# Adding a saved residual into an image in SBUF: accumulating DMAs in place of loads and engine additions

## The chip, the cores and the metric

The kernel runs on one core of one Trainium2 chip. The metric is device time in microseconds (us) of one execution of the whole program. The core has TensorE (PE in the profile, with its weight loads as PEld), VectorE (DVE), ScalarE (ACT), GpSimd (POOL) and SyncE (SP), and 16 DMA engines. Every array here is float32.

## The reference, cut to what matters

The image x is 4 x 48 x 128 x 128 (batch, channels, rows, columns). Four layers follow each other, each on a group-normalised copy of x and added to x:

```python
x = x + attention(_gn(x), ...)      # layer 0
x = x + scans(_gn(x), down1, right1, left1)   # layer 1
x = x + scans(_gn(x), down2, right2, left2)   # layer 2
x = x + gated_mlp(_gn(x), ...)      # layer 3

def step(w, b):                     # one step of a scan
    def f(carry, inp):
        nxt = inp + conv1d(carry, w, b)     # 5 taps, 48 -> 48 channels
        return (nxt, nxt)
    return f
# scans: down over the rows, up, right over the columns, left: 127 steps each
# _gn: 16 groups of 3 channels, mean and variance over channels, rows and columns
```

What matters here is the place between layer 1 and layer 2. The scans of layer 1 leave their output in the image; `x` from before layer 1 is then added to it, the sum is kept for the residual of layer 2, and its group statistics and normalisation feed the scans of layer 2.

## The kernel before

**Layout.** `image` is one SBUF tensor of 128 partitions by 32768 float32 columns. The 48 channels sit twice in it: partitions 0 to 47 (`LO`) hold one half of the pixels (even columns or rows), partitions 64 to 111 (`HI`) the other. Partitions 48 to 63 are a gap that holds zeros. The columns fall into four parts of `IMG` = 8192 columns, numbered t = 0 to 3. Parts 0 and 1 together hold batch elements 0 and 1, parts 2 and 3 hold batch elements 2 and 3. A part is four chunks of `CHUNK` = 2048 columns (`PER` = 4).

**DRAM copies.** `saved[0]` holds x from before layer 1. It is written while layer 0 ends, and its DMAs (L381, L388) are waited for before anything reads it. `saved[1]` receives x from before layer 2 and is read back, block by block, after the scans of layer 2 (L431, L539 and the DVE loop at the end of the scans).

**Between the scan layers.** Each engine runs its own instruction list and waits on semaphores. Layer 1 ends with the last swap copies on DVE (L1220). Then:

- SP loads `saved[0]` chunk by chunk into four buffers `back[0..3]` in the tensor `work` (`bring`, L398: two DMAs of 384 KiB a chunk, one for `LO`, one for `HI`). The four chunks of part 0 are loaded early, during the scans of layer 1. A chunk of part t+1 is loaded once the addition of the same chunk of part t has freed its buffer.
- DVE adds chunks 0 and 1 of each part (L1230), GpSimd adds chunks 2 and 3 (L529). Additions count into `s_kept_v` and `s_kept_p`.
- DVE takes the statistics of each part: 16 instructions of 512 columns (L1047, `take_stats`), the last four of them behind GpSimd's second addition. After parts 0 and 1, and again after parts 2 and 3, `group_norm` turns statistics into scale and shift: aggregation on DVE (L1054), two small matmuls (L805), a square root on ACT (L600) and a few small DVE instructions up to `gn_shift` (L1068).
- SP stores each part to `saved[1]` (`save_columns`, L403): parts 0 to 2 whole, two DMAs of 1536 KiB each, part 3 in two halves of two DMAs of 768 KiB each. SP works in program order, so the store of part t is issued behind the loads of part t+1.
- ACT (L695) and DVE (L1251) normalise the image in place, each part only once its store has landed (`s_save`). ACT takes parts 0 and 1 and most of part 3, DVE takes part 2 and the first quarter of part 3. Then PE starts the scans of layer 2 (L923).

Before the first load, SP waits for `s_back_gap`: four memsets of the gap lanes of `back` on GpSimd (L497), done during the scans of layer 1.

Of the kernel before, what the change touches and what calls it, by code (L numbers as in the profile page):

```python
# [97 lines left out]
def build(nc, x, qkv_t, v_w, dw_t, dw_v, proj_t, temp, scan_w, scan_b,  # L98
          w1, b1, gamma, beta, gdw, gdw_b, gpw_t, gpw_b, w2, b2,
          ident_c, group_half_c, group_flat_c, saved, flat, out):  # L100
    with ExitStack() as ctx:
# [114 lines left out]
        s_gate_w = sem("s_gate_w")  # L216
        s_back_gap = sem("s_back_gap")
        s_gate_zero = sem("s_gate_zero")
# [35 lines left out]
        s_back = [sem(f"s_back{i}") for i in range(PER)]  # L254
        s_kept_v = sem("s_kept_v")
        s_kept_p = sem("s_kept_p")
        s_res = sem("s_res")
# [80 lines left out]
        def _(sp):  # L338
# [53 lines left out]
            for i in range(PARTS):  # L392
                sp.wait_ge(s_part[i], 32)
            sp.wait_ge(s_back_gap, PER)

            def bring(c):
                for half, rows in enumerate((LO, HI)):
                    sp.dma_start(back[c % PER][rows, :],  # L398
                                 saved[0][half, :, c * CHUNK:(c + 1) * CHUNK]).then_inc(s_back[c % PER], 16)

            def save_columns(b, c0, c1):
# [3 lines left out]

            for c in range(PER):
                bring(c)
            for b in range(NB - 1):
                for m in range(PER):
                    if m < VCH:  # L410
                        sp.wait_ge(s_kept_v, b * VCH + m + 1)
                    else:
                        sp.wait_ge(s_kept_p, b * (PER - VCH) + m - VCH + 1)
                    bring((b + 1) * PER + m)
                save_columns(b, 0, IMG)
            sp.wait_ge(s_kept_v, NB * VCH)
            save_columns(NB - 1, 0, VCH * CHUNK)
            sp.wait_ge(s_kept_p, NB * (PER - VCH))
            save_columns(NB - 1, VCH * CHUNK, IMG)
            for t in range(NB):  # L420
# [43 lines left out]
        def _(pool):  # L464
# [29 lines left out]
            for g in range(2):  # L494
                pool.wait_ge(s_state[g], 1)
            for m in range(PER):
                nc.gpsimd.memset(back[m][32:HALF, :], 0.0).then_inc(s_back_gap, 1)  # L497
            pool.wait_ge(s_back_gap, PER)

            pool.wait_ge(s_const, 16 * N_CONST)  # L500
# [22 lines left out]
            for g in range(2):  # L523
                pool.wait_ge(s_state[g], PASSES * STEPS + 1)
            with pool.Fori(0, NB) as b:
                for m in range(VCH, PER):
                    pool.wait_ge(s_back[m], b * 32 + 32)
                    dst = image[0:P, ds(b * IMG + m * CHUNK, CHUNK)]
                    nc.gpsimd.tensor_tensor(dst, dst, back[m], ALU.add).then_inc(s_kept_p, 1)  # L529

# [3 lines left out]
            with pool.Fori(0, NB // 2) as bp:  # L534
                with pool.Fori(0, NBLK // PER) as q:
                    for m in range(PER):
                        pool.wait_ge(s_back[m], bp * (NBLK * 8) + q * 32 + (32 * NB + 32))
                        pool.wait_ge(s_flat[m % 2], bp * (NBLK * 16) + q * 64 + (m // 2 * 32 + 32))
                        natural(nc.gpsimd, bp, q, m, 1, 1).then_inc(s_res_p, 1)  # L539
# [499 lines left out]
        def _(dve):  # L1039
# [182 lines left out]
            for layer in range(2):  # L1222
                if layer:
                    for pair in range(2):
                        for s in range(2):
                            t = 2 * pair + s
                            for m in range(VCH):
                                dve.wait_ge(s_back[m], t * 32 + 32)
                                dst = image[0:P, t * IMG + m * CHUNK:t * IMG + (m + 1) * CHUNK]
                                v.tensor_tensor(dst, dst, back[m], ALU.add).then_inc(s_kept_v, 1)  # L1230
                            for m in range(PER):
                                if m < VCH:
                                    dve.wait_ge(s_kept_v, VCH * t + (m + 1))
                                else:
                                    dve.wait_ge(s_kept_p, (PER - VCH) * t + (m - VCH + 1))
                                for q in range(2):
                                    for c in range(2):
                                        k0 = (2 * m + c) * BLK
                                        src = img(slice(0, P), 2 * pair + q, s, slice(k0, k0 + BLK), slice(0, J2))
                                        last = take_stats(P, 2 * pair + q, s * NBLK + 2 * m + c,  # L1240
                                                          src.rearrange("p k j -> p (k j)"))
                            last.then_inc(s_stat, 1)
                        if pair == 0:
                            dve.wait_ge(s_stat, X_STATS + NB + 2)
                            group_norm(4, P, NSTAT, 0, 2)
# [50 lines left out]
            with dve.Fori(0, NB // 2) as bp:  # L1296
                with dve.Fori(0, NBLK // PER) as q:
                    for m in range(PER):
                        dve.wait_ge(s_back[m], bp * (NBLK * 8) + q * 32 + (32 * NB + 32))
                        dve.wait_ge(s_flat[m % 2], bp * (NBLK * 16) + q * 64 + (m // 2 * 32 + 32))  # L1300
# [150 lines left out]
```

## Time and profile before

| | before |
|---|---|
| median of 3 runs | 2922.65 us (2920.05 to 2925.99) |
| the profiled execution | 2917.19 us |
| its span, first to last instruction | 2915.4 us |
| mean granted TensorE clock | 0.937 |
| PE busy | 2487.5 us (85%) |
| DVE busy | 1630.1 us (56%) |
| ACT busy | 1095.3 us (38%) |
| POOL busy | 250.1 us (9%) |
| moved by DMA | 130.12 MB |

"Busy" is the time in which an engine executes instructions. The span is one profiled execution, and all durations and moments below are taken from it, counted from the span's start. In a view of windows the columns are the window, its length, busy time and number of instructions for PE, PEld, DVE, ACT and POOL, the granted TensorE clock (1.00 is 2.4 GHz, 0.50 is 1.2 GHz), the mean busy share of the 16 DMA engines, and the GB/s that they moved. A share slightly above 1 comes from packets whose recorded times overlap.

### The profile page before, as it was taken

What the parts mean: (1) busy time and instruction counts of PE and PEld (TensorE: products, weight loads), DVE (VectorE), ACT (ScalarE), POOL (GpSimd) and SP (SyncE); (2) the same over time, 40 slices, a digit from 0 to 9 for tenths busy, and PEclk for the clock granted to TensorE, in tenths of its full rate; (3) what the DMA queues carried; (4) which work ended last, traced back from release to release, by engine and by line L of the source; (5) the groups of instructions that cost most, each with busy time, mean ns of one, the idle gap of its engine ahead of it and who ended that gap; (6) DMA issues with size and microseconds to landing.
All of it is one profiled execution on the core that took longest, in us unless ns stands there. A gap on an engine that the chain in (4) does not pass through costs nothing.

```text
span 2915.4 us, 46645 instructions
## 1 busy us (share of the span) xinstructions
PE 2487.5 (85%) x18076; PEld 2175.9 (75%) x18076; DVE 1630.1 (56%) x3797; ACT 1095.3 (38%) x2617; POOL 250.1 (9%) x244
## 2 busy tenths in 40 slices
PE   2999999999999899999999906999999998005876
PEld 2989949949943699999999906999999998002443
DVE  2323223223232455885568875558855788776564
ACT  3533353353357344444444423444444444002221
POOL 1000000000000440000000040000000000454110
PEclk9999999999999999999999957999999999558898
DMA  8840000003001400000000094000000000683223
GB/s 147 146 74 2 1 1 1 1 0 88 1 0 44 87 1 1 2 1 1 1 1 1 1 249 97 1 1 1 1 1 1 1 2 1 192 283 87 87 86 87
DMA packets 51667, 130.12 MB, mean 45 GB/s; under 512 B 9121, under 2 KB 34049, under 8 KB 44897
## 3 DMA queue, kind: packets, MB, share of 16 engines
q1 hardware_dynamic: 48352, 113.92, 16.4%
q10 hardware_dynamic: 2976, 13.34, 1.6%
q8 instruction: 138, 2.26, 0.3%
q14 instruction: 73, 0.59, 0.1%
q0 software_dynamic: 128, 0.01, 0.0%
HBM read 76.91 MB, written 50.33 MB: 44 GB/s over the span
## 4 chain that ended last, share of the span: by engine, by line
PE 83%; DVE 6%; DMA 6%; issue 2%; ACT 1%; SPq 0%; POOL 0%; DVEq 0%; ACTq 0%; POOLq 0%
PE bank L923 17%; PE bank L924 15%; PE bank L926 15%; PE bank L830 13%; PE bank L884 11%; PE bank L845 3%; PE bank L835 3%; DMA flat_rows<-work 2%; PE bank L968 2%; DVE work L322 1%; PE bank L1026 1%; DMA work<-saved 1%; DMA work<-in_x 1%; DVE stats L1047 1%; PE bank L959 1%
## 5 line engine op out<-in xcount | busy, mean ns | idle before, releaser
L1210 DVE TENSOR_SCALAR bank<-image,scan_bias 112x128 f32<-112x128 f32 x2032 | 725.7, 358 | 416.0 <-ACT image L714 373.1
L714 ACT COPY image<-bank 112x128 f32<-112x128 f32 x2032 | 596.5, 294 | 787.7 <-PE bank L926 787.4
L923 PE MATMUL bank<-image,scan_wt 112*112 112x128 f32 x4064 | 818.2, 282 | 31.3 <-ACT image L695 16.4
L924 PE MATMUL bank<-image,scan_wt 112*112 112x126 f32 x4064 | 770.7, 271 | 0.0
L926 PE MATMUL bank<-image,scan_wt 112*112 112x126 f32 x4064 | 769.6, 270 | 0.0
L923 PEld LDWEIGHTS bank<-image,scan_wt 112*112 112x112 f32 x4064 | 556.2, 175 | 41.9 <-ACT image L695 26.9
L924 PEld LDWEIGHTS bank<-image,scan_wt 112*112 112x112 f32 x4064 | 581.3, 176 | 0.0
L926 PEld LDWEIGHTS bank<-image,scan_wt 112*112 112x112 f32 x4064 | 578.3, 176 | 0.0
L621 ACT ACTIVATE work<-image,gn_shift,gn_scale 48x567 f32<-48x567 f32 (+5 forms) x384 | 332.5, 899 | 344.6 <-PE bank L835 219.3
L830 PE MATMUL bank<-work 112*128 112x192 f32 x2304 | 424.0, 332 | 10.1 <-issue 10.1
L830 PEld LDWEIGHTS bank<-work 112*128 112x128 f32 x2304 | 375.3, 193 | 11.7 <-issue 11.2
L884 PE MATMUL bank<-work 112*112 112x512 f32 x768 | 331.3, 593 | 3.0 <-DVE work L1137 3.0
L884 PEld LDWEIGHTS bank<-work 112*112 112x112 f32 x768 | 135.3, 177 | 192.9 <-issue 189.6
L1105 DVE COPY work<-bank 128x384 f32<-128x384 f32 x128 | 71.3, 557 | 359.9 <-PE bank L835 276.7
L1047 DVE BATCH_NORM_STATS2 stats<-image 112x6 f32<-112x512 f32 (+2 forms) x240 | 152.9, 683 | 62.1 <-ACT image L593 43.7
L1158 DVE TENSOR_TENSOR image<-image,bank 112x512 f32<-112x512 f32 (+1 forms) x64 | 44.1, 689 | 236.7 <-PE bank L884 140.6
L805 PE MATMUL bank<-mean_var,group_flat 128*128 128x4 f32 x2 | 0.6, 366 | 165.4 <-DVE mean_var L1054 165.4
L322 POOL TENSOR_TENSOR work<-image,work 48x1024 f32<-48x1024 f32 x16 | 58.8, 3680 | 777.3 <-DVE image L1220 715.2
L805 PEld LDWEIGHTS bank<-mean_var,group_flat 128*128 128x128 f32 x2 | 0.5, 313 | 165.6 <-DVE mean_var L1054 165.6
L805 PE MATMUL bank<-mean_var,group_half 112*112 112x2 f32 (+2 forms) x12 | 2.5, 276 | 136.3 <-DVE mean_var L1054 136.3
L322 DVE TENSOR_TENSOR work<-image,work 48x1024 f32<-48x1024 f32 x48 | 98.6, 2053 | 28.1 <-DMA flat_rows<-work 26.5
L845 PE MATMUL bank<-work 128*96 128x96 f32 x1024 | 108.2, 248 | 3.8 <-DVE work L1105 3.8
(137 smaller groups left out, 1604.3 us busy)
## 6 DMA issues: line engine op xcount, KB each, us to landing
work<-saved SPq DMA_DIRECT2D x64, 384.0 KB, 8.5
saved<-image SPq DMA_DIRECT2D x10, 1536.0 KB, 21.7
flat_rows<-work ACTq DMA_DIRECT2D x32, 384.0 KB, 7.4
image<-flat_rows SPq DMA_DIRECT2D x4, 3072.0 KB, 14.3
out<-image SPq DMA_DIRECT2D x8, 1536.0 KB, 8.1
saved<-image SPq DMA_DIRECT2D x12, 768.0 KB, 10.1
band<-in_x SPq DMA_DIRECT2D x16, 384.0 KB, 5.9
work<-in_x SPq DMA_DIRECT2D x16, 384.0 KB, 6.1
```

The lines of the kernel that those rows point to most:

```text
L322: return eng.tensor_tensor(o[:, :, :, :, half], i0.rearrange("p g s k j -> p (g s) k j"), i1, ALU.add)
L621: last = nc.scalar.activation(dst.rearrange("p (k j) -> p k j", j=J2)[:, :, d[0]:d[1]], src, ACT.Identity, bias=gn_shift[part, b:b + 1], s ...
L714: nc.scalar.copy(line(g, along_w, at), state_bank(g, done)).then_inc(s_state[g], 1)
L830: last = mm(dst, (blk_z, blk_n)[buf][n % 2][:, o:o + 2 * J2], qk_w[buf][:, dy].rearrange("p a b -> p (a b)"), start=(t == 0), stop=(packed ...
L835: last = mm(dst[:, side * QK:(side + 1) * QK], blk_2[n % 2][:, side, sub, o:o + 2 * J2], qk_w2[:, side, :], start=False, stop=(side == 1))
L845: last = mm(bank_gram[0:QK, 0:QK], v, v, start=(i == 0 and c == 0), stop=(i == PAIRS - 1 and c == 3))
L884: last = mm(bank_out[sub][0:P, :], out_w[buf][:, dy, :], (blk_z, blk_n)[buf][n % 2][:, o:o + BLK * J2], start=(t == 0), stop=(t == len(pro ...
L923: mm(dst, wt[:, 1], src, start=False, stop=False, skip_group_check=True)
L924: mm(dst[:, 1:J2, :], wt[:, 0], src[:, 0:J2 - 1, :], start=False, stop=False, skip_group_check=True)
L926: mm(dst[:, 0:J2 - 1, :], wt[:, 2], src[:, 1:J2, :], start=False, stop=True, skip_group_check=True).then_inc(s_prod[g], 1)
L1047: return v.bn_stats(stat6[0:parts, b, ds(c * 6, 6)], src)
L1210: v.tensor_scalar(state_bank(g, done), line(g, along_w, src), scan_bias[:, 3 * layer + kind:3 * layer + kind + 1], None, ALU.add).then_inc ...
```

## The change

The loads of `saved[0]` into `back`, the additions on DVE and GpSimd, their semaphores and the memsets of the gap lanes are gone. In their place GpSimd issues 16 accumulating DMAs, all behind each other and without a wait between them, once layer 1 has ended: for each part t, for each half u of it (4096 columns), one for `LO` and one for `HI`. Each has `saved[0]` in DRAM as its source and the image in SBUF as its destination, adds the source to what stands there, and is 48 partitions x 4096 columns (768 KiB), cut into rows of 2048 elements (8192 bytes). Each half counts on its own semaphore `s_acc[2t+u]`. DVE waits for a half before the eight statistics instructions on it. SP waits for both halves of a part and stores it to `saved[1]`; part 3 is stored half by half, as before in two DMAs each. Since `bring` no longer counts on `s_back`, the later waits on it lose the term `32 * NB`.

```diff
--- before.py
+++ after.py
@@ -214,7 +214,6 @@
 
         s_const = sem("s_const")
         s_gate_w = sem("s_gate_w")
-        s_back_gap = sem("s_back_gap")
         s_gate_zero = sem("s_gate_zero")
         s_gate_const = sem("s_gate_const")
         s_pool = sem("s_pool")
@@ -252,8 +251,7 @@
         s_swap = sem("s_swap")
         s_tail = sem("s_tail")
         s_back = [sem(f"s_back{i}") for i in range(PER)]
-        s_kept_v = sem("s_kept_v")
-        s_kept_p = sem("s_kept_p")
+        s_acc = [sem(f"s_acc{i}") for i in range(2 * NB)]
         s_res = sem("s_res")
         s_res_p = sem("s_res_p")
         s_flat = [sem(f"s_flat{i}") for i in range(2)]
@@ -391,32 +389,18 @@
                 sp.wait_ge(s_save[t], 32)
             for i in range(PARTS):
                 sp.wait_ge(s_part[i], 32)
-            sp.wait_ge(s_back_gap, PER)
-
-            def bring(c):
-                for half, rows in enumerate((LO, HI)):
-                    sp.dma_start(back[c % PER][rows, :],
-                                 saved[0][half, :, c * CHUNK:(c + 1) * CHUNK]).then_inc(s_back[c % PER], 16)
-
             def save_columns(b, c0, c1):
                 for half, rows in enumerate((LO, HI)):
                     sp.dma_start(saved[1][half, :, b * IMG + c0:b * IMG + c1],
                                  image[rows, b * IMG + c0:b * IMG + c1]).then_inc(s_save[b], 16)
 
-            for c in range(PER):
-                bring(c)
-            for b in range(NB - 1):
-                for m in range(PER):
-                    if m < VCH:
-                        sp.wait_ge(s_kept_v, b * VCH + m + 1)
-                    else:
-                        sp.wait_ge(s_kept_p, b * (PER - VCH) + m - VCH + 1)
-                    bring((b + 1) * PER + m)
-                save_columns(b, 0, IMG)
-            sp.wait_ge(s_kept_v, NB * VCH)
-            save_columns(NB - 1, 0, VCH * CHUNK)
-            sp.wait_ge(s_kept_p, NB * (PER - VCH))
-            save_columns(NB - 1, VCH * CHUNK, IMG)
+            for t in range(NB):
+                for u in range(2):
+                    sp.wait_ge(s_acc[2 * t + u], 32)
+                    if t == NB - 1:
+                        save_columns(t, u * IMG // 2, (u + 1) * IMG // 2)
+                if t < NB - 1:
+                    save_columns(t, 0, IMG)
             for t in range(NB):
                 sp.wait_ge(s_save[t], saves(1, t))
 
@@ -493,10 +477,6 @@
 
             for g in range(2):
                 pool.wait_ge(s_state[g], 1)
-            for m in range(PER):
-                nc.gpsimd.memset(back[m][32:HALF, :], 0.0).then_inc(s_back_gap, 1)
-            pool.wait_ge(s_back_gap, PER)
-
             pool.wait_ge(s_const, 16 * N_CONST)
             pool.wait_ge(s_gate_w, 16 * N_GATE)
             n = 0
@@ -522,11 +502,17 @@
             pool.wait_ge(s_swap, 6 * K2)
             for g in range(2):
                 pool.wait_ge(s_state[g], PASSES * STEPS + 1)
-            with pool.Fori(0, NB) as b:
-                for m in range(VCH, PER):
-                    pool.wait_ge(s_back[m], b * 32 + 32)
-                    dst = image[0:P, ds(b * IMG + m * CHUNK, CHUNK)]
-                    nc.gpsimd.tensor_tensor(dst, dst, back[m], ALU.add).then_inc(s_kept_p, 1)
+            for t in range(2):
+                pool.wait_ge(s_save[t], 32)
+            for i in range(PARTS):
+                pool.wait_ge(s_part[i], 32)
+            for t in range(NB):
+                for u in range(2):
+                    for half, rows in enumerate((LO, HI)):
+                        dst, src = (r[:, t * IMG + u * IMG // 2:t * IMG + (u + 1) * IMG // 2]
+                                    for r in (image[rows, :], saved[0][half]))
+                        pool.dma_start(dst.rearrange("p (a n) -> p a n", n=CHUNK), src.rearrange("p (a n) -> p a n", n=CHUNK),
+                                       accum_op=ALU.add, max_dma_last_dim=8192).then_inc(s_acc[2 * t + u], 16)
 
             pool.wait_ge(s_swap, 2 * 6 * K2)
             for g in range(2):
@@ -534,7 +520,7 @@
             with pool.Fori(0, NB // 2) as bp:
                 with pool.Fori(0, NBLK // PER) as q:
                     for m in range(PER):
-                        pool.wait_ge(s_back[m], bp * (NBLK * 8) + q * 32 + (32 * NB + 32))
+                        pool.wait_ge(s_back[m], bp * (NBLK * 8) + q * 32 + 32)
                         pool.wait_ge(s_flat[m % 2], bp * (NBLK * 16) + q * 64 + (m // 2 * 32 + 32))
                         natural(nc.gpsimd, bp, q, m, 1, 1).then_inc(s_res_p, 1)
 
@@ -1224,15 +1210,9 @@
                     for pair in range(2):
                         for s in range(2):
                             t = 2 * pair + s
-                            for m in range(VCH):
-                                dve.wait_ge(s_back[m], t * 32 + 32)
-                                dst = image[0:P, t * IMG + m * CHUNK:t * IMG + (m + 1) * CHUNK]
-                                v.tensor_tensor(dst, dst, back[m], ALU.add).then_inc(s_kept_v, 1)
                             for m in range(PER):
-                                if m < VCH:
-                                    dve.wait_ge(s_kept_v, VCH * t + (m + 1))
-                                else:
-                                    dve.wait_ge(s_kept_p, (PER - VCH) * t + (m - VCH + 1))
+                                if m % 2 == 0:
+                                    dve.wait_ge(s_acc[2 * t + m // 2], 32)
                                 for q in range(2):
                                     for c in range(2):
                                         k0 = (2 * m + c) * BLK
@@ -1296,7 +1276,7 @@
             with dve.Fori(0, NB // 2) as bp:
                 with dve.Fori(0, NBLK // PER) as q:
                     for m in range(PER):
-                        dve.wait_ge(s_back[m], bp * (NBLK * 8) + q * 32 + (32 * NB + 32))
+                        dve.wait_ge(s_back[m], bp * (NBLK * 8) + q * 32 + 32)
                         dve.wait_ge(s_flat[m % 2], bp * (NBLK * 16) + q * 64 + (m // 2 * 32 + 32))
                         for a, half in ((0, 0), (0, 1), (1, 0)):
                             last = natural(v, bp, q, m, a, half)
```

## Rows read from the trace of the kernel before

**Rows 1.** The page: PE's busy line, and PE and DMA in 40 slices.

```profile
PE 2487.5 (85%) x18076; PEld 2175.9 (75%) x18076; DVE 1630.1 (56%) x3797; ACT 1095.3 (38%) x2617; POOL 250.1 (9%) x244
...
PE   2999999999999899999999906999999998005876
...
DMA  8840000003001400000000094000000000683223
```

**Rows 2.** Windows: scans of layer 1, the stretch between the layers.

```profile
1000.00:1600.00 600.00, 597.65 (x5329) 594.55 (x5328) 403.53 (x1189) 255.97 (x889) 53.68 (x100) 1.00 0.02 3
...
1673.40:1777.90 104.50, 2.14 (x8) 1.79 (x8) 72.70 (x99) 22.72 (x9) 41.43 (x8) 0.51 0.83 219
```

**Rows 3.** The chain that ended last, 1697 to 1778 us: start, length, what.

```profile
1697.81 22.16 DMA work<-saved
...
1729.26 17.58 DMA work<-saved
...
1751.50 4.50 POOL image L529
...
1756.38 14.79 DMA saved<-image
...
1774.33 3.07 ACT image L695
...
1777.94 0.74 PE bank L923 x2
```

**Rows 4.** Waits from 1660 to 1790 us: waiting line, releaser, total, times, longest.

```profile
POOL image L529 <- DMA work<-saved: 39.4, 3, 16.3
ACT image L695 <- DMA saved<-image: 26.8, 2, 17.5
...
DVE image L1230 <- DMA work<-saved: 13.3, 4, 8.0
```

**Rows 5.** Windows inside the stretch, and one of stores alone (668 to 692 us).

```profile
1677.00:1688.70 11.70, 0.00 (x0) 0.00 (x0) 11.70 (x11) 0.00 (x0) 10.91 (x2) 0.50 0.72 138
1684.00:1752.00 68.00, 1.07 (x4) 0.90 (x4) 49.17 (x72) 16.13 (x5) 28.58 (x7) 0.50 0.98 266
...
1720.00:1730.00 10.00, 0.00 (x0) 0.00 (x0) 9.51 (x13) 0.63 (x1) 7.38 (x2) 0.50 1.05 333
...
668.00:692.00 24.00, 24.00 (x184) 23.85 (x183) 9.11 (x23) 6.94 (x9) 0.00 (x0) 1.00 0.79 184
```

**Rows 6.** Groups of instructions from 1674 to 1778 us: busy us, mean ns.

```profile
L529 POOL TENSOR_TENSOR image<-image,work 112x2048 f32 x8 | 41.4, 5197 | 653.7 <-DVE image L1220 614.3 <-DMA work<-saved 39.4
L1047 DVE BATCH_NORM_STATS2 stats<-image 112x6 f32<-112x512 f32 x64 | 38.7, 676 | 5.8 <-POOL image L529 5.7
L1230 DVE TENSOR_TENSOR image<-image,work 112x2048 f32<-112x2048 f32 x8 | 22.4, 2824 | 13.3 <-DMA work<-saved 13.3
```

**Rows 7.** Loads of line 398 in the stretch: durations ns, first and last start.

```profile
L398 SPq DMA_DIRECT2D work<-saved x24: 302/614/4041, 1677.1 to 1735.3; - x24
```

**Rows 8.** Timeline: start, length, instruction, idle time before it.

```profile
1675.15 12.77 POOL L529 TENSOR_TENSOR image<-image,work 112x2048 f32 x2 [614.29 <-DVE image L1220]
...
1756.03 2.47 DVE L1047 BATCH_NORM_STATS2 stats<-image 112x6 f32<-112x512 f32 x4 [1.99 <-POOL image L529]
1758.54 1.03 DVE L1054 BATCH_NORM_AGGREGATE mean_var<-stats 112x2 f32<-112x96 f32 x2
...
1762.20 0.16 DVE L1068 SCALAR_TENSOR_TENSOR gn_shift<-gn_mean,gn_scale 112x2 f32<-112x2 f32 x1
```

**Rows 9.** GpSimd's timeline where it issues four small DMAs.

```profile
2610.83 0.71 POOL L548 DMA_DIRECT2D work<-in_w  x1 [0.72 <-POOL work L546]
2611.53 0.53 POOL L549 DMA_DIRECT2D work<-in_w  x1
2612.06 0.50 POOL L550 DMA_DIRECT2D work<-in_b  x1
```

**Rows 10.** DMA issues, whole span: count, KB each, median us to landing.

```profile
scan_wt<-in_scan_w SPq DMA_DIRECT2D x60, 9.0 KB, 1.7
...
work<-in_w POOLq DMA_DIRECT2D x2, 3.0 KB, 6.3
```

## The prediction, made before the changed kernel was run

> **What bounds the kernel now.** I read the page first, to see where PE is not busy, since PE carries the kernel: 85% busy, with full slices through both groups of scans and one hole near slice 24, where the DMA row stands at 9 and 4 [rows 1]. A window over the scans of layer 1 shows PE busy for 597.65 of 600 us and the DMA engines at 0.02 [rows 2]. The change touches nothing that runs there but memsets and early loads that PE does not wait for. So only the hole counts. It lasts from 1673.4 to 1777.9 us, 104.5 us in which PE does 2.14 us of work [rows 2].
>
> The second question is what fills the hole. DVE is busy for 72.7 us of it and POOL for 41.4, but the DMA engines for 0.83 of the whole [rows 2], and for 0.98 from 1684 to 1752 us, at 266 GB/s [rows 5]. The waits say the same: POOL waited 39.4 us for loads, DVE 13.3 us, and ACT 26.8 us for stores [rows 4]. The chain of waits through the hole runs over two loads of 22.16 and 17.58 us, a last addition on POOL that ends at 1751.50 + 4.50 = 1756.0, a store of 14.79 us, ACT's normalisation, and PE's start at 1777.94 [rows 3]. The reader is to see that the DMA engines are the bound of this stretch and that the additions are not.
>
> The bytes confirm it. 24 loads fall in the stretch [rows 7], each 384 KiB or 0.393 MB, together 9.44 MB; the four chunks of part 0 (3.15 MB) were loaded before it. The stores are 4 parts of 3.15 MB, 12.58 MB, of which three parts (9.44 MB) belong ahead of the last addition. 9.44 + 9.44 = 18.9 MB at 266 GB/s is 71 us, nearly all of the 81 us from 1675 to 1756.
>
> **The change part by part.**
>
> 1. It removes 8 additions on DVE, 22.4 us, and 8 on POOL, 41.4 us [rows 6]. They lie beside transfers. DVE's share never comes back as time unless the DMA engines get less to do, so I give the two nothing by themselves.
>
> 2. It removes 24 loads in the stretch, 9.44 MB, and adds 16 accumulating DMAs, 12.58 MB, all in the stretch: nothing can be fetched ahead, since the destination is the image that the scans still write. That alone is 3.15 MB more, 3.15/0.266 = 11.8 us.
>
> 3. The price of an accumulated byte is not in the trace. An accumulating DMA must read DRAM, read SBUF, add and write SBUF. From below it is one transfer, as a load is: 266 GB/s as in the saturated stretch [rows 5], or 333 GB/s as in its best 10 us [rows 5]. From above it is three passes (two reads and one write, none overlapped), each at 266 GB/s. I take two transfers, a load and a store of the same bytes, since that is what it does to SBUF; and since such traffic runs in both directions at once, I take for it the mixed window, 333 GB/s: 2 x 12.58 / 0.333 = 75.6 us. Reads in one direction alone run slower here: loads alone moved 138 GB/s at a share of 0.72, stores alone 184 at 0.79, which is some 190 and 230 GB/s if the engines were full [rows 5]. The three parts stored ahead of the last accumulation cost 9.44 / 0.266 = 35.5 us. Together 111.1 us of DMA time.
>
> The Trainium skill ("Collectives: The Full Stack", "Why ReduceScatter is half of AllGather") says that a DMA add is slowed not by the adding but by its two source reads, which share one ring, so that a reduce runs at half the rate of a copy. No row here shows an accumulate. By that rule on the 266 GB/s row the accumulations would take 12.58 / 0.133 = 94.6 us and the sum below would be 19 us more.
>
> 4. GpSimd now issues the DMAs. The additions on POOL began at 1675.15 [rows 8], so the first issue falls there. Issuing a small one took 0.71, 0.53 and 0.50 us [rows 9]; 16 of them at under 3 us each would be under 48 us, beside 111 us of transfers, so issue is hidden. But a small DMA from POOL took 6.3 us to land against 1.7 from SP [rows 10]. Those 4.6 us stand once at the front, where nothing covers them: before, the first chunks were already in SBUF. So the transfers begin at 1675.15 + 4.6 = 1679.8. SP waits for the last accumulation of a part before it stores it; later accumulations do not queue behind SP, so that wait holds back nothing but the store.
>
> 5. The last accumulation then lands at 1679.8 + 111.1 = 1790.9, against 1756.0 for the last addition: +34.9 us.
>
> 6. The tail. Before it was 1777.94 - 1756.0 = 21.9 us, with the store of 14.79 us in it [rows 3]. Now two things are different. DVE takes eight chunks of statistics after the last landing instead of four: 8 x 0.61 (2.47/4 in [rows 8]) = 4.9 us, and from the aggregation to gn_shift it is 1762.36 - 1758.54 = 3.8 us [rows 8], together 8.7, still under 14.8. And the earlier stores have had more time to drain, so that the last 1.57 MB may land faster than in 14.8 us, by at most 14.8 - 8.7 = 6.1. I take 3 us off.
>
> 7. The statistics of a part take 16 x 0.6 = 10 us, under the 28 us that a part's DMA work now takes; they stay hidden, also the group norm of parts 0 and 1 and ACT's first normalisation, which wait for stores that land long before the end. The four removed memsets and the early loads lie under the scans [rows 2]: nothing.
>
> Sum: +34.9 - 3 = +32 us in the hole. The profiled execution took 2917.19 us, the span and 1.8 us around it, and the median of the runs is 2922.65. I add the difference to the median: 2922.65 + 32 = 2954.7, say **2955 us**. Its own range: all the work at 333 GB/s gives 34.6/0.333 = 103.9 us and +22 with the full 6 us of the tail; all at 266 gives 130.1 us and +54 with none of it: 2944 to 2977 us.
>
> **The rivals.**
>
> - *One pass.* The accumulation costs what a load costs: 22.0 MB at 266 GB/s is 82.8 us, landing at 1762.6, +6.6 - 3 = +3.6 us, **2926 us**. For it: a load is short of the engines' full rate for some other reason than the reading (loads alone give only some 190 GB/s at a full share), so a second read might hide under it. Against it: the engines' recorded share was 0.98 already.
>
> - *One pass and better overlap: faster.* Two queues, POOL's and SP's, feed the engines at once, with transfers of 768 KiB and no stop to wait for a buffer. If one-pass accumulations and stores then ran at 333 GB/s throughout, 22.0/0.333 = 66.1 us, landing at 1745.9, -10.1 - 3 = -13 us, **2910 us**. It decides where the stores and accumulations together take under 76.2 us (1756.0 - 1679.8): with the stores at 266, where accumulated bytes run above 12.58/(76.2 - 35.5) = 309 GB/s. For it: the 10 us at 333. Against it: every byte is read twice, and the average of the saturated stretch is 266.
>
> - *Three passes.* The two reads and the write follow each other in each engine: 37.7/0.266 = 141.9 us, with the stores 177.4, landing at 1857.2: +101 - 3 = +98 us, **3021 us**. For it: loads alone, one partition half at a time, got only 138 GB/s; the accumulations go in that order too, a `LO` and then a `HI`, on one queue. Against it: nothing in the trace shows reads and writes in an engine excluding each other, and the mixed window is the fastest.
>
> - *GpSimd's issue sets the pace.* 16 DMAs would need over 7 us each. Against it the three rows at 0.5 to 0.7 us; it is within the chance of the slow case.
>
> **How the numbers follow.** Two transfers 50%, three passes or slower accumulation of other cause (+60 us and more) 25%, one pass 14%, faster 11%. Measurement tells apart about 0.2%, 5.8 us: faster is below 2916.8, slower above 2928.5. The faster case gives 0.11. The one-pass case is mostly within the bound: 0.12. The rest is slower: 0.77. The range leaves out the best of the faster case and the worst of the slow one: 2915 to 3025 us.
>
> **What would show it.** In the changed kernel's profile: the hole in PE some 136 us long, DMA share near 1 for over 100 us of it; DVE's busy time in the hole down from 72.7 to about 50 us, its idle time before L1047 put down to DMA; 16 issues on POOL of a few us at most; the last accumulation landing near 1791 us and PE's start some 19 us behind. The first landing tells the most: the first half of part 0 (1.57 MB) alone on the engines should land some 10 to 13 us after its issue. Under 9 us speaks for one pass, over 17 us for three. I am wrong if the accumulations do not fill the engines' time (a latency per row instead of a rate), if POOL's issues last 7 us or more, or if the stores and accumulations slow each other beyond the sum of their shares.

## The result and the profile after

The changed kernel takes 2975.03 us (median of 4 runs, 2961.16 to 2981.57) against 2923.1 us before (4 runs): a ratio of 1.0173 with a 95% interval of 1.0148 to 1.0198, which is 50.6 us more (43 to 58). The forecast was 2955 us and slower: the direction held, the extra time was 50.6 us where 32 were forecast, and the mechanism held in part. The profiled execution is the fastest of the four, 2961.16 us with a span of 2959.4, 44 us over the one before.

The page shows where the time went (PE and DMA in 40 slices, then two DMA queues with packets, MB and their share of 16 engines over the span). The rows of before are in [rows 1].

```profile
PE   2989999999999899999999603999999999005786
...
DMA  8830000012002100000000396000000000683222
...
q1 hardware_dynamic: 46304, 101.33, 14.5%
q0 software_dynamic: 1920, 12.59, 2.3%
```

The hole in PE near slice 24 is wider. 12.59 MB now go over GpSimd's queue (q0), which carried almost nothing before. Windows over the hole and its parts, with the columns of [rows 2]:

```profile
1674.70:1824.60 149.90, 2.13 (x8) 1.81 (x9) 49.71 (x88) 22.62 (x8) 14.93 (x16) 0.50 0.85 174
...
1679.00:1807.00 128.00, 1.07 (x4) 0.90 (x4) 36.08 (x65) 15.97 (x5) 10.63 (x12) 0.50 0.87 182
1679.00:1755.00 76.00, 1.07 (x4) 0.90 (x4) 21.54 (x41) 7.49 (x3) 10.63 (x12) 0.50 1.03 203
1755.00:1807.00 52.00, 0.00 (x0) 0.00 (x0) 14.54 (x24) 8.48 (x3) 0.00 (x0) 0.50 0.63 150
```

DVE's busy time falls from 72.7 us in [rows 2] to 49.7, as it should. The DMA engines move 182 GB/s while accumulations and stores share them, where loads and stores moved 266 [rows 5]. Their share is 1.03 in the first 76 us and only 0.63 in the last 52 us before the last landing; the prediction wanted it near 1 for over 100 us, and the hole 136 us long where it is 149.9. The waits from 1660 to 1830 us (the rows of before are [rows 4]):

```profile
DVE stats L1033 <- DMA image<-saved: 95.3, 8, 16.3
ACT image L681 <- DMA saved<-image: 15.3, 2, 13.1
```

DVE's and GpSimd's timelines, and the end of the chain of waits (start, length, what). The trace gives no name to an accumulation's landing there, "an unknown queue":

```profile
1674.69 14.93 POOL L514 DMA_DIRECT2D image<-saved  x16 [621.89 <-DVE image L1206]
...
1690.31 4.84 DVE L1033 BATCH_NORM_STATS2 stats<-image 112x6 f32<-112x512 f32 x8 [16.27 <-DMA image<-saved]
...
1807.15 4.84 DVE L1033 BATCH_NORM_STATS2 stats<-image 112x6 f32<-112x512 f32 x8 [13.42 <-DMA image<-saved]
```

```profile
1791.57 15.56 another core or an unknown queue
...
1807.50 10.03 DMA saved<-image
...
1820.94 3.14 ACT image L681
...
1824.61 0.74 PE bank L909 x2
```

Issuing all 16 DMAs cost GpSimd 14.93 us, 0.9 each. The first rows start moving at 1676.5, 1.8 us behind the first issue. The first half landed 15.6 us after its issue (1690.31 - 1674.69), the last at 1807.1 against 1756.0 for the last addition [rows 3], and PE starts 17.5 us behind that.

### The profile page after: what moved, and what is told of

Same layout as the page of the kernel before. It is cut to its first block, busy times and chain, and to the rows that moved or that the text cites. A ratio compares the mean times of both kernels' runs of the same rounds, so it can differ in the third digit from the quotient of the medians.

```text
span 2959.4 us, 46594 instructions
## 1 busy us (share of the span) xinstructions
PE 2491.4 (84%) x18076; PEld 2177.8 (74%) x18076; DVE 1608.3 (54%) x3789; ACT 1095.8 (37%) x2617; POOL 219.2 (7%) x248
## 3 DMA queue, kind: packets, MB, share of 16 engines
q0 software_dynamic: 1920, 12.59, 2.3%
## 4 chain that ended last, share of the span: by engine, by line
PE 82%; DVE 5%; DMA 5%; another core or an unknown queue 3%; issue 2%; ACT 1%; SPq 1%; POOL 0%; DVEq 0%; ACTq 0%; POOLq 0%
PE bank L909 17%; PE bank L910 15%; PE bank L912 15%; PE bank L816 13%; PE bank L870 11%; PE bank L831 3%; PE bank L821 3%; DMA flat_rows<-work 2%; PE bank L954 2%; DVE work L320 1%; PE bank L1012 1%; DMA work<-in_x 1%; PE bank L945 1%; DMA image<-saved 1%
```

## The experiments

Each was timed against the kernel before on the same chip; the third column is the ratio's excess times that kernel's median. "Last landing" is when the last residual data are in place in the profiled execution: the last load-fed addition, copy or accumulation. The last two columns come from one execution each, the others from 4 to 12 executions of a changed version. From PE's start to the end that execution took 1137.5 us before and between 1125 and 1152 us in the others, so stages behind the hole move the total by as much as some of the effects below.

| run | ratio (95% interval) | us against before | last landing | PE starts |
|---|---|---|---|---|
| before | 1 | 0 | 1756.0 | 1777.9 |
| changed kernel | 1.0173 (1.0148 to 1.0198) | +50.6 | 1807.1 | 1824.6 |
| plain copies, GpSimd | 1.0072 (1.0045 to 1.0100) | +21.1 | 1781.1 | 1798.5 |
| plain copies, ScalarE | 1.0069 (1.0044 to 1.0093) | +20.1 | 1778.1 | 1795.5 |
| plain copies, SP, one queue | 1.0117 (1.0093 to 1.0140) | +34.2 | 1767.5 | 1806.0 |
| paced accumulations | 1.0163 (1.0131 to 1.0195) | +47.7 | 1804.6 | 1822.1 |
| no stores | 0.9963 (0.9950 to 0.9976) | -10.8 | 1755.3 | 1771.1 |
| stores last | 1.0186 (1.0160 to 1.0213) | +54.3 | 1756.8 | 1828.1 |
| before without early loads | 1.0034 (1.0015 to 1.0052) | +9.9 | 1768.5 | 1795.5 |
| part 0 by engines, rest accumulated | 1.0128 (1.0099 to 1.0156) | +37.4 | 1793.2 | 1810.6 |
| changed kernel, 112 partitions | 1.0135 (1.0113 to 1.0157) | +39.4 | 1806.5 | 1822.4 |
| before, six buffers | 0.9983 (0.9967 to 0.9999) | -5.0 | 1748.5 | 1769.8 |
| before, 112 partitions | 0.9972 (0.9956 to 0.9987) | -8.2 | 1752.5 | 1772.6 |
| before, both | 0.9977 (0.9954 to 1.0000) | -6.7 | 1743.8 | 1764.9 |

**Plain copies in place of the accumulations.**

```diff
-  accum_op=ALU.add, max_dma_last_dim=8192).then_inc(s_acc[2 * t + u], 16)
+  max_dma_last_dim=8192).then_inc(s_acc[2 * t + u], 16)
```

> The 16 DMAs on GpSimd keep their shapes, order and semaphores but copy instead of adding, so the image loses the scans' sum here. Double-read theory: an 8192-byte row of an accumulation took 629 ns at the median in the changed kernel, a plain one needs about half when alone (309 ns was the 5th percentile of the loads before) and 528 ns at the median beside stores. The engines' time on them falls from 68.6 to 40 to 52 us, and the kernel gets 16 to 28 us faster than the changed one, near +25 to +35 us over before. Rival, drift alone: the add is free and the whole loss is that the 16 DMA engines run apart with no wait to hold them together; then this run is within 5 us of the changed kernel, +45 to +55 us over before. A third: everything is in the doubled read; then it comes within 10 us of before.

Measured +21.1 us (13 to 29), 29.5 us below the changed kernel: in time the doubled-read theory, a little over its upper end. "Drift alone" falls. Its window up to the last landing:

```profile
1679.00:1781.00 102.00, 1.06 (x4) 0.89 (x4) 36.08 (x65) 16.20 (x5) 4.25 (x8) 0.50 0.93 224
```

Copies and stores together moved 224 GB/s, where accumulations and stores moved 182 in the changed kernel.

Share times length is the time in which an engine is busy, on average: 0.87 x 128 = 111 us in the changed kernel, 0.93 x 102 = 95 us here. So of the 26 us between the two last landings some 17 are busy time and 9 idle.

The theory wanted the engines' time on the 16 DMAs to fall from 68.6 us to 40 to 52. It fell to 60. In views of the DMA queues the last figure of q0 is its share of 16 engines' time in the window, first for the changed kernel (1674.7 to 1824.6 us), then for this run (1674.2 to 1798.5):

```profile
q0 software_dynamic: 1792, 12.58, 46.0%
...
q0 software_dynamic: 1792, 12.58, 48.6%
```

That is 0.460 x 149.9 = 69 us and 0.486 x 124.3 = 60 us. The single 8192-byte packets (rows) show it too. The shortest took 307 ns as a plain copy (before and here) and 628 ns as an accumulation, just double. But more than half of the accumulated rows took 628 or 629 ns, while the median of the copied ones was 607: some 900 in the first 23 us, before a store ran beside them, and 540 beside stores. The Trainium skill ("Collectives: The Full Stack", "Why ReduceScatter is half of AllGather") puts a reduce at half a copy's rate for its two reads; the shortest rows agree, the transfers as a whole do not, as the runs without stores and with one queue show below.

**Paced accumulations.**

```diff
                 for u in range(2):
+                    if 2 * t + u >= 2:
+                        pool.wait_ge(s_acc[2 * t + u - 2], 32)
                     for half, rows in enumerate((LO, HI)):
```

> As the changed kernel, but GpSimd issues a half only after the half two before it has landed, so at most two halves (3.15 MB) are in flight. Drift theory: in the changed kernel the 16 engines finish the last half up to 66 us apart and the DMA share falls to 0.63 in the last 52 us; with the engines held together the share stays near 0.95 and the last landing comes 10 to 20 us earlier: +32 to +42 us over before. Rival, rate alone (the slow engines are slow whatever the others do, since their share of the rows is fixed): each half lands when its slowest engine is done, pacing gains nothing and the gap before each next half (about 4 us from issue to the first bytes) can even cost: +50 to +65 us.

+47.7 us (38 to 57), the last landing at 1804.6 instead of 1807.1. But here the first issue came 2.1 us earlier too (1672.55), so from it to the last landing it took 132.1 us against 132.4. In the trace's completion records the engines of the changed kernel really come apart. Each half counts 32 completions, and between its first and its last pass, in us, for the eight halves:

```
changed kernel    8.0 12.5 21.3 34.8 40.2 45.1 55.2 66.0
no stores         8.5 10.6 12.9 17.2 18.4 18.9 19.1 18.9
112 partitions    2.4  2.4 12.1 10.4 29.8 25.9 36.4 40.8
```

Pacing holds them together (23 us apart in the last half instead of 66) and raises the DMA share in the late window (1755 to 1804.6 us, against 0.63 in the changed kernel), and it gains nothing:

```profile
1755.00:1804.60 49.60, 0.00 (x0) 0.00 (x0) 13.84 (x23) 7.98 (x2) 3.11 (x4) 0.50 0.80 169
```

So the drift theory falls. The reading that fits is that the idle engines had finished early and the end waits for slow ones that a wait does not hurry.

**No stores.** The ten stores to the second DRAM copy become semaphore increments, and the residual of layer 2 is read from the first copy.

```diff
-  sp.dma_start(saved[1][half, :, b * IMG + c0:b * IMG + c1],
-               image[rows, b * IMG + c0:b * IMG + c1]).then_inc(s_save[b], 16)
+  sp.sem_inc(s_save[b], 16)
...
-  kept_rows = saved[1][half].rearrange(...)
+  kept_rows = saved[0][half].rearrange(...)
```

> As the changed kernel, but the ten stores to the second DRAM copy are left out (the residual of layer 2 is then taken from the first copy, so the output lacks a part). Double-read theory: 1536 rows at 629 ns on 16 engines are 60 us, so the last landing comes 60 to 68 us after the transfers begin, near 1743 us, and the tail shrinks to 9 + 7 us: the kernel ends 15 to 20 us BEFORE the old one (-20 to -10 us). Drift theory adds: even alone, the accumulations let the engines drift, the slowest is 10 to 25 us behind the mean and the kernel comes out at -5 to +10 us. If the slow engines are slow because of stores only, no drift shows.

-10.8 us (-15 to -7), inside the first theory's -20 to -10. Its landing was not: 1743 expected, 1755.3 measured, with the completions of the last half 19 us apart, as the drift theory says. The issues begin at 1676.99 here, so the accumulations alone took 78.3 us to the last landing. The first row moves at 1678.8. The third line is the queue's share from 1677.0 to 1771.1 us:

```profile
1676.99 14.93 POOL L513 DMA_DIRECT2D image<-saved  x16 [622.18 <-DVE image L1205]
...
1755.27 4.85 DVE L1032 BATCH_NORM_STATS2 stats<-image 112x6 f32<-112x512 f32 x8 [2.19 <-DMA image<-saved]
...
q0 software_dynamic: 1792, 12.58, 72.2%
```

That is 1.8 us of start, where the prediction has 4.6, and 76.5 of transfer, near its 75.6. Of the 76.5 the average engine was busy for 0.722 x 94.1 = 68 us; the rest is waiting for the slowest. In the changed kernel the same way from first issue to last landing took 132.4 us: the stores cost 54.1 us. The engines' time on the accumulations hardly changed (68 us here, 69 there).

**Stores last.**

```diff
-            for t in range(NB):
-                for u in range(2):
-                    sp.wait_ge(s_acc[2 * t + u], 32)
+            for i in range(2 * NB):
+                sp.wait_ge(s_acc[i], 32)
+            for t in range(NB):
+                for u in range(2):
```

> The changed kernel, but SP begins the stores only after the last accumulation has landed. Contention theory: beside stores the last accumulation landed at 1807 us, without them at 1755; 12.58 MB of stores alone at 230 to 246 GB/s are 51 to 55 us, so PE starts near 1755 + 53 + 7 = 1815: stores and accumulations gain nothing by running together, and this run is 5 to 12 us below the changed kernel, +40 to +47 us over before. Rival (they do overlap, and serial order loses that): 10 to 25 us above the changed kernel.

+54.3 us (47 to 62), not told apart from the changed kernel's +50.6, and above the 40 to 47 expected. The two windows hold accumulations alone and stores alone:

```profile
1679.00:1756.80 77.80, 1.06 (x4) 0.90 (x4) 36.08 (x65) 0.20 (x1) 11.57 (x13) 0.50 0.85 159
1757.00:1821.00 64.00, 1.07 (x4) 0.90 (x4) 11.55 (x19) 15.96 (x5) 0.00 (x0) 0.50 0.82 197
```

From the first issue (1675.6) to the last store's landing (1821.3) are 145.7 us one after the other; in the changed kernel the two together took 142.8 (1674.7 to 1817.5). Running accumulations beside stores gains 3 us, so the contention theory holds for the transfers, though the time did not come down as it said. Plain copies of the same shape gain far more. Alone, 12.58 MB of them would take 85 us (at 148 GB/s, from the run with one queue below) and the stores 64, together 149 us; run beside each other on GpSimd's queue and SP's they took 117 (1674.2 to 1791.4).

**Before, without the early loads.**

```diff
+            sp.wait_ge(s_swap, 6 * K2)
+            for g in range(2):
+                sp.wait_ge(s_state[g], PASSES * STEPS + 1)
             for c in range(PER):
                 bring(c)
```

> The kernel before, but the four chunks of part 0 are loaded only once layer 1 has ended. It prices the loss of the early loads, one term of the prediction. Theory: 3.15 MB more in the stretch at 266 GB/s are 11.8 us and the first landing about 5 us that nothing covers, partly in the same time: +10 to +16 us over before. Rival (the engines were not really the bound in the first 12 us, with a share of 0.72): only the first wait shows, +5 to +7 us.

+9.9 us (4 to 15), at the lower end of the theory; the interval reaches into the rival too. In its profiled execution the last landing comes 12.5 us later than before and PE's start 17.5, more than the median shows.

**Plain copies from ScalarE's queue, and from SP's.** In the first, ScalarE waits for the end of layer 1 and issues the 16 copies. In the second, SP does it on the queue of its stores:

```diff
+            copy(0)
+            copy(1)
             for t in range(NB):
                 for u in range(2):
                     sp.wait_ge(s_acc[2 * t + u], 32)
+                    if u == 1 and t + 2 < NB:
+                        copy(t + 2)
```

> As the run with plain copies in place of accumulations (the scans' sum is lost), but ScalarE issues them on its hardware queue instead of GpSimd. It asks what of the 21 us over before that the plain copies still cost is due to GpSimd's queue. If its later start (15 us to the first landing) and descriptors made by GpSimd matter: 4 to 10 us less, +11 to +17 us over before. If only the lost early loads (9.9 us) and the stores' competing with the loads on a second queue matter: +18 to +24, the same as on GpSimd's queue.

> Plain copies in place of the accumulations again (the scans' sum is lost), issued by SP on the queue of the stores and one part ahead of them, as the loads of the kernel before are. On a queue of their own the copies cost 20 us over before (GpSimd's and ScalarE's alike), of which 9.9 us are the lost early loads. If the other 11 us come from the stores taking turns with the copies on a second queue: +8 to +13 us over before. If they come from the larger transfers or the missing buffer: +18 to +22 us.

ScalarE's copies cost +20.1 us (13 to 27), GpSimd's +21.1: which of the two engines issues them makes no difference that these runs can tell. SP's single queue did worse than either theory, +34.2 us (27 to 41). Taking turns with the stores on a second queue was not the loss but a gain. The last copy lands at 1767.5, earlier than on GpSimd's queue, but the stores are left for the end and PE starts 38.5 us behind it. The window of its start, and the queue's packets, MB and share in the same window: for 45 us copies run alone, with the engines' share at 1.00, at 148 GB/s.

```profile
1674.30:1719.00 44.70, 0.00 (x0) 0.00 (x0) 14.53 (x24) 0.00 (x0) 0.00 (x0) 0.51 1.00 148
...
q1 hardware_dynamic: 937, 6.63, 100.2%
```

Those 6.63 MB are 809 rows of 8192 bytes (the other packets are a few bytes each), so a row held its engine for 16 x 44.7 / 809 = 0.88 us, where the shortest took 0.307. A share of 1.00 is thus not the most that the engines can do; the rows spend most of their time waiting for something that the trace does not name. Accumulated rows without stores took 0.63 us at the median, and a half of them landed every 9.0 us (1692.2 to 1755.2) where a half of plain copies landed every 10.6 (1687.1 to 1740.1; on GpSimd's queue 10.5, 1688.0 to 1698.5; all from completion records). Alone, then, accumulating was a little faster than copying.

**Part 0 by engines, the rest accumulated.** Part 0 is loaded early and added by DVE; GpSimd accumulates parts 1 to 3, paced.

```diff
-            for t in range(NB):
+            for t in range(1, NB):
...
+                            for m in range(0 if t else PER):
+                                dve.wait_ge(s_early[m], 32)
+                                dst = image[0:P, m * CHUNK:(m + 1) * CHUNK]
+                                v.tensor_tensor(dst, dst, back[m], ALU.add).then_inc(s_acc[m // 2], 1)
```

> Part 0 as in the kernel before (loaded early into four buffers, here added by DVE alone), parts 1 to 3 by accumulating DMAs, each half issued once the half two before it has landed. Theory of three terms (doubled read, lost early loads, contention with the stores): the accumulations shrink by a quarter, from 78 to 59 us when alone, and the first store starts 25 us earlier: 20 to 28 us below the changed kernel, +22 to +30 us over before. Rival, a fixed cost of the accumulating path however little goes over it: +40 us or more.

+37.4 us (29 to 46), between the two theories. PE starts 14 us earlier than in the changed kernel. A quarter less to accumulate gave less than hoped, since the stores cost no less: the accumulations took from 1674.1 to 1793.2 us, 119 us, where three quarters of the 78.3 us without stores are 59.

**112 partitions in one DMA.** Each pair of 48-partition DMAs between the layers becomes one that spans both halves and the gap lanes; in both kernels the stores of `saved[0]` at the end of layer 0 change in the same way. Where a semaphore counted 32 for a pair, SP adds 16 first.

```diff
-                for half, rows in enumerate((LO, HI)):
-                    sp.dma_start(saved[1][half, :, b * IMG + c0:b * IMG + c1],
-                                 image[rows, b * IMG + c0:b * IMG + c1]).then_inc(s_save[b], 16)
+                sp.sem_inc(s_save[b], 16)
+                sp.dma_start(saved[1][:, b * IMG + c0:b * IMG + c1],
+                             image[0:P, b * IMG + c0:b * IMG + c1]).then_inc(s_save[b], 16)
```

> The changed kernel, but each pair of DMAs (partitions 0 to 47, then 64 to 111) between the layers becomes one DMA of 112 partitions, which also carries the 16 gap lanes (zeros): 17% more bytes, 7 rows for each of the 16 engines where the pair gave 3 and 3. Theory of the SBUF side: with 48 partitions some engines share their way into SBUF (in the run without stores the fastest engine did its 96 rows at 629 ns each, 60 us, the slowest took 79 us), and a transfer over both halves evens it out: 112 rows at 629 ns are 70 us for the accumulations however many others run, stores speed up too, and the kernel comes out 15 to 30 us below the changed one (+20 to +35 us over before). Rival, the engines' own time is the bound: 17% more bytes, 15 to 20 us above the changed kernel.  By the first the landings of one DMA also lie closer together.

> The same edit in the kernel before: loads, stores between the layers and the stores of layer 0 as single DMAs of 112 partitions. SBUF-side theory: 22.0 MB become 25.7 MB, but at 350 GB/s or more instead of 266 the stretch sheds 8 to 12 us: -6 to -14 us against before. Rival, the engines' own time: 25.7/0.266 = 97 us against 83, +10 to +14 us.

In the changed kernel it gave +39.4 us (33 to 46), 11 us below the pairs and short of the expected 15; in the profiled execution PE starts only 2 us earlier, so most of those 11 us lies outside the hole (the stores of layer 0 changed too) or in the spread of the runs, and the intervals of the two runs overlap. The first two halves, without stores beside them, show what was expected: their completions lie 2.4 us apart. Once stores run, the engines come apart again, to 41 us in the last half instead of 66, so the partitions explain at most part of the drift. In the kernel before it gave -8.2 us (-13 to -4), the lowest median of the versions that compute the whole result, though not told apart from the two that follow. The rival, engines bound by their bytes, falls. With 17% more bytes the saturated stretch moved 316 GB/s, where [rows 5] has 266:

```profile
1684.00:1752.00 68.00, 1.06 (x4) 0.89 (x4) 65.09 (x73) 16.20 (x5) 33.06 (x7) 0.50 0.94 316
```

Without the gap lanes the 316 are 271 GB/s of image, 2% over the 266, and PE starts 5 us earlier than before. So the window does not carry all of the 8.2 us. The profiled execution was the slowest of the ten, 7 us over the one before; what the wide DMAs do behind the hole is open.

The Trainium skill ("SBUF — State Buffer", "Can I just issue two DMAs to hit both halves?") says that only one transfer over all partitions reaches every port into SBUF, and that two DMAs for the two halves are not joined. The two windows agree in direction, 266 GB/s in pairs and 316 wide with the gap lanes counted.

**Six buffers, alone and with wide DMAs.** The two buffers `nat` join the four of `back`, so six chunks are loaded during layer 1's scans.

```diff
+        ring = back + nat
...
-            for c in range(PER):
+            for c in range(PER + 2):
                 bring(c)
```

> The kernel before, with six buffers for the loaded residual instead of four (the two that idle until the end of the scans of layer 2 join in), so six of the 16 chunks are loaded during the scans of layer 1. If DMA bytes in the stretch are the bound: 1.57 MB less at 266 GB/s, 5.9 us less, and fewer stops of POOL for loads: -4 to -8 us against the kernel before. The measured price of the four early chunks (+9.9 us without them) would give half of that, -5 us. Rival (the stores and the tail set the end): within 2 us.

> Six buffers and 112-partition DMAs together in the kernel before, the late loads of the residual of layer 2 included. If the SBUF-side theory holds: -5 us of the six buffers, -6 to -14 us of the wider DMAs, -2 to -5 us in the last stretch before the MLP: -12 to -24 us. If it doesn't: +5 to +15 us.

-5.0 us (-10 to 0) alone, as expected. Together with wide DMAs everywhere -6.7 us (-13 to 0), less than the -12 to -24 expected and not told apart from the wide DMAs alone. In its trace PE does start 13 us earlier than before, but from there to the end it takes 1152.1 us against 1137.5, and why is open.

## Why the prediction was right, and where its size was off

- **DMA is the bound of the hole, the additions are not** (what bounds the kernel, step 1). Right. DVE lost 23 us of work, GpSimd all its additions, and the hole grew. Moving transfers out of the stretch shortened the old kernel (six buffers, -5.0 us), moving them into it lengthened it (+9.9 us). But the prediction took the engines' recorded share for the engines' capacity, and it is not that: 148 GB/s at 1.00, 266 at 0.98, and 316 at 0.94 with wide DMAs. For the same reason its estimate for loads alone, some 190 GB/s if the engines were full, did not hold: copies alone moved 148 at a full share.
- **3.15 MB more in the stretch, 11.8 us** (step 2). 9.9 us measured (4 to 15), first wait included.
- **An accumulated byte costs two transfers** (step 3, the accumulation term, 75.6 us). The size was right, 76.5 us alone, and one pass at 266 GB/s (47 us) and three passes (142 us) both fall. The reason holds only in the shortest rows, 628 ns against 307. Alone, plain copies moved 148 GB/s and accumulations 159: accumulating cost nothing over copying, and it was the transfer alone, without loads and stores mixed, that ran far below 266. That twice the bytes at 333 GB/s came out at the measured time is in part luck. The price of the add to the kernel, 29.5 us between accumulations and plain copies, comes up only beside the stores.
- **The stores ahead of the last accumulation, 9.44 MB at 266 GB/s, 35.5 us** (step 3, the store term). This is the term that was mis-sized. The stores delayed the last landing by 54.1 us. Two things were off. The 266 GB/s was the rate of loads and stores mixed; stores alone moved 197. And the first half of part 3 is stored before the second half has landed, so by 1807.1 us 11.0 MB of stores had moved (the sum of their packets) and not 9.44. 11.0 MB at 197 GB/s are 56 us, close to the 54.1: the accumulations and the stores cost what each costs alone. The old kernel's mix was fast because loads and stores overlap: 9.44 MB of loads at 148 GB/s and 12.58 MB of stores at 197 are 64 + 64 = 128 us apart, and took 94 us together (from 1677.1 to 1771.2, [rows 7] and [rows 3]). Plain copies kept that gain (117 us for 149), accumulations lost it (143 for 146). An accumulation both reads and writes SBUF, which could explain it, but no run shows what the two share.
- **Issue and start** (step 4). Issue was hidden, at 0.9 us each. The 4.6 us of start, taken from a small DMA's way to landing, were 1.8. Whether GpSimd or ScalarE issued the copies made no difference (21.1 against 20.1 us).
- **The sign of the first landing.** It came after 15.6 us, over the 10 to 13 given. By the prediction's own terms two transfers give 4.6 + 3.15/0.333 = 14.0 us, one pass 10.5 and three passes 22, so the bounds of 9, 10 to 13 and 17 did not follow from them. Nor could it tell an add from a copy: the plain copies' first half landed after 13.8 us (1674.2 to 1688.0).
- **The landing at 1790.9** (step 5) was 1807.1, late by 16.2 us: 18.6 from the stores and 0.9 from the accumulations, less 2.8 of start and 0.5 of an earlier issue. **The tail** (step 6) was 17.5 us against the 18.9 forecast, since the last store landed in 10.0 us.
- **From the hole to the forecast.** PE started 14.8 us later than forecast (1824.6 against 1809.8). The extra time was 50.6 us against 32, and those 18.6 us are also the store term's error. That the two agree is luck: the other terms of the hole gave 4 us back, and the rest lies in the spread of the runs.
- **The rivals.** The faster case asked for accumulated bytes above 309 GB/s; they ran at 159 alone. GpSimd's issue was far from its point of decision.

The plain copies leave 21 us over before: 9.9 of them are the lost early loads. For the other 11, the issuing engine and turn-taking with the stores are out. That the first 1.57 MB of copies now run with nothing beside them, as the single queue showed in the large, is likely but was not tested apart. Open as well is why some engines are slow beside stores: neither pacing nor evening out the partitions removed it.

## What to carry to other kernels

An accumulating DMA takes the addition off a compute engine; it does not make the transfer cheaper. What it cost here lay in the company: plain copies overlapped with stores on a second queue and accumulations did not. So compare it with the copy in the mix in which it will run. When a transfer is priced from a window in which loads and stores run together, ask which direction the new mix has, and price each kind by a window of its own. Do not read a DMA share of 1.00 as the most that the engines can move; look at how long one row takes against the shortest row. Look at how many partitions one DMA spans before looking for another way to move the same bytes: with one of 112 partitions for two of 48, gap lanes and all, both kernels had lower medians, by 8 and by 11 us, the second with overlapping intervals.

## What the runs showed of the hardware that was not expected

- Plain copies into 48 partitions alone kept the engines' share at 1.00 at only 148 GB/s, 0.88 us a row; accumulations of the same shape reached 159 GB/s.
- Beside stores a copied row took less of its engine's time than alone (540 against some 900 ns at the median), an accumulated row the same (629 ns).
- Accumulations and stores on two queues drive the 16 DMA engines apart: by the eighth half, its first and last completion lay 66 us apart, and 19 us without the stores.
- Letting the DMA engines catch up with each other (two halves in flight at most) changed the way from first issue to last landing by 0.3 us of 132.
